# A graph layer on Trainium2: all chunks of the adjacency split in two parts, and the order of the engines' work changed

## What is computed

```python
h = jnp.maximum(_layernorm(x, axis=-1), 0.0)
A_fwd = [adj, adj, shifted]                      # shifted: identity rolled by one row
A_list = A_fwd + [transposed each] + [eye]       # 7 relations; shifted and eye are the same for all batches
HW  = einsum('bnf,rfo->rbno', h, W[:, :F]) + einsum('rd,rdo->ro', W_edges, W[:, F:])[:, None, None, :]
AHW = einsum('rbnm,rbmo->rbno', A, HW)
out = x + max(AHW over r) + b
```

## Time and profile before

| | us |
|---|---|
| median of 3 runs | 216.88 |
| lowest and highest | 216.61, 218.16 |
| profiled execution | 216.98 |
| its span (first to last instruction) | 215.3 |
| busy: TensorE, VectorE, ScalarE, GpSimd | 206.3, 177.0, 160.8, 95.9 |

### The profile page before, as it was taken

How to read it: one execution, slowest core, us unless ns; L and a number is a source line. 1 busy time by engine, 2 the same in 40 slices (tenths; PEclk the granted TensorE clock), 3 DMA queues, 4 the chain that set the end, 5 groups by cost and what they waited for, 6 DMA issues and landing times.

```text
span 215.3 us, 3420 instructions
## 1 busy us (share of the span) xinstructions
PE 206.3 (96%) x902; PEld 149.5 (69%) x902; DVE 177.0 (82%) x414; ACT 160.8 (75%) x431; POOL 95.9 (45%) x140
## 2 busy tenths in 40 slices
PE   7799779999999999999999999999999999999994
PEld 7456456777767777777767777776777777777772
DVE  3574997988889797988989798888979798888755
ACT  3779788697896969698796969689696969876220
POOL 3112946446172735527082644617273552718200
PEclk9999979999999999999999999999999999999998
DMA  5999995376693939678492938769393938610101
GB/s 175 313 345 370 376 362 199 108 292 245 202 336 93 380 79 313 215 253 283 156 355 69 374 127 295 241 198 335 86 384 89 342 130 253 234 53 0 50 0 49
DMA packets 31587, 47.14 MB, mean 219 GB/s; under 512 B 1632, under 2 KB 11088, under 8 KB 31568
## 3 DMA queue, kind: packets, MB, share of 16 engines
q1 hardware_dynamic: 31568, 46.92, 64.3%
HBM read 42.72 MB, written 4.19 MB: 218 GB/s over the span
## 4 chain that ended last, share of the span: by engine, by line
PE 84%; SPq 6%; DMA 5%; DVE 2%; issue 1%; ACT 1%; POOL 0%; DVEq 0%; ACTq 0%; POOLq 0%
PE bank_p L761 11%; PE bank_p L763 10%; PE bank_p L762 9%; PE bank_g L725 6%; PE bank_gT L704 6%; PE bank_g L730 5%; PE bank_g L729 5%; PE bank_g L736 5%; DMA adj_sb<-in_adj_dram 5%; PE bank_gT L716 5%; PE bank_gT L710 5%; PE bank_gT L709 4%; PE bank_p L751 3%; PE bank_p L679 3%; PE bank_p L671 3%; PE bank_g L762 2%
## 5 line engine op out<-in xcount | busy, mean ns | idle before, releaser
L321 POOL TENSOR_TENSOR a_lo<-adj_sb,a_hi 128x512 fp32r<-128x512 f32 x15 | 19.4, 1295 | 72.3 <-DVE h_lo L548 68.5
L579 DVE TENSOR_TENSOR best<-bank_p,best 128x512 f32<-128x512 f32 x48 | 33.2, 691 | 8.4 <-PE bank_p L763 7.3
L434 ACT ACTIVATE gT_hi<-bank_gT 128x512 fp32r<-128x512 f32 x16 | 9.6, 598 | 30.9 <-PE bank_gT L716 30.5
L576 DVE SCALAR_TENSOR_TENSOR best<-bank_p,c_col,best 128x512 f32<-128x512 f32 x32 | 24.0, 750 | 5.8 <-ACT best L453 5.1
L389 ACT ACTIVATE a_hi<-adj_sb 128x512 fp32r<-128x512 f32 x45 | 27.7, 620 | 1.3 <-DMA adj_sb<-in_adj_dram 1.3
L402 ACT ACTIVATE aT_hi<-adjT_sb 128x512 fp32r<-128x512 f32 x45 | 27.7, 620 | 0.0
L315 POOL TENSOR_TENSOR o_sb<-best,x_bias 128x512 f32<-128x512 f32 x15 | 20.0, 1332 | 15.8 <-DVE best L579 15.8
L418 ACT ACTIVATE h<-x_sb,shift,rstd 128x128 f32<-128x128 f32 x60 | 24.7, 497 | 1.4 <-DVE shift L528 1.4
L542 DVE TENSOR_TENSOR aT_lo<-adjT_sb,aT_hi 128x512 fp32r<-128x512 f32 x30 | 24.5, 854 | 0.0
L729 PE MATMUL bank_g<-aT_hi,h_hi 128*128 128x512 f32 x45 | 24.4, 541 | 0.0
L709 PE MATMUL bank_gT<-a_hi,h_hi 128*128 128x512 f32 x45 | 23.6, 525 | 0.0
(11 more groups left out here) (110 smaller groups left out, 501.8 us busy)
## 6 DMA issues: line engine op xcount, KB each, us to landing
adj_sb<-in_adj_dram SPq DMA_DIRECT2D x15, 1024.0 KB, 5.6
adjT_sb<-in_adjT_dram SPq DMA_DIRECT2D x15, 1024.0 KB, 5.6
xT_sb<-in_xT_dram SPq DMA_DIRECT2D x16, 256.0 KB, 5.9
x_sb<-in_x_dram SPq DMA_DIRECT2D x15, 256.0 KB, 6.1
out_dram<-o_sb SPq DMA_DIRECT2D x15, 256.0 KB, 5.9
adj_sb<-in_adj_dram SPq DMA_DIRECT2D x4, 256.0 KB, 3.4
adjT_sb<-in_adjT_dram SPq DMA_DIRECT2D x4, 256.0 KB, 4.8
w_sb<-in_W_dram SPq DMA_DIRECT2D x3, 128.0 KB, 4.5
```

Of the source, the lines that this page charges most:

```text
L579: op = nc.vector.tensor_tensor(best[q][:, :], product, best[q][:, :], ALU.max)
```

## The change

Chunk 0 is split as the others are: four chunks of a_hi, a_lo, aT_hi, aT_lo, h_hi and h_lo, and no float32 matmul from batch 1 on. VectorE makes two of the four low parts, GpSimd two. The copy into `summed` is gone for batches from 1 on; the same copy with its accumulator now writes a_hi. Then the order changes:
- TensorE does turn_sums behind aggregate, and the leading sums of the last batch's last product, in two halves, in begin_products.
- ScalarE makes sumsT behind g_hi. In batch 1 it does split_adj(2) behind the maximum's first term.
- VectorE does gT_lo and hT_lo ahead of a_lo(b+1). Batches 0 and 1 have an order of their own.
- GpSimd does part_sums(b+1) behind aT_lo(b+1), and finish(b-1) behind that.
- In batch 0 the layer norm goes in halves, the second half of x is loaded from ScalarE's queue, and the first aggregation comes ahead of the transposes.
- SP asks for adj and adjT of batch 2 before the second xT, and for x of batch 3 behind them.

```diff
-WHOLE = (0,)
-SPLIT = (1, 2, 3)
-NS = len(SPLIT)
-ND = NS - 1
+ND = 2
+NG = 2
+NS = ND + NG
-WARM_UP = 10
+WARM_UP = 9
...
             load_xT(0)
+            load_adj(2)
+            load_adjT(2)
             load_xT(1)
-            for b in range(B):
+            load_x(3)
+            for b in range(1, B):
+                if b + 1 < B:
+                    load_xT(b + 1)
                 if b + 3 < B:
                     load_x(b + 3)
                 if b + 2 < B:
                     load_adj(b + 2)
-                if b > 0:
-                    store(b - 1)
+                store(b - 1)
                 if b + 2 < B:
                     load_adjT(b + 2)
-                    load_xT(b + 2)
...
             split_adj_last(1)
             add_bias(0)
+            part_sums(1)
             split_adjT_last(1)
+            finish(0)
             add_bias(1)
             for b in range(1, B):
-                part_sums(b)
-                finish(b - 1)
+                if b >= 2:
+                    finish(b - 1)
                 if b + 1 < B:
...
                     split_adjT_last(b + 1)
+                    part_sums(b + 1)
...
+                if 2 <= b < B - 1:
+                    split_adj(b + 1)
                 split_gT(b)
                 split_hT(b)
-                copy_sumsT(b)
                 if b + 1 < B:
                     make_h(b + 1)
                 split_g(b)
+                copy_sumsT(b)
                 begin_best(b)
+                if b == 1:
+                    split_adj(b + 1)
...
             split_g_lo(0)
-            take_best(0, 1)
             split_h_lo(1)
             variance(2)
+            take_best(0, 1)
+            split_adj_lo(1)
             take_best(0, 2)
-            split_adj_lo(1)
+            scale_and_shift(2)
             for i in range(NH, NPROD):
                 take_best(0, i)
...
+            for c in range(C):
+                pe.wait_ge(ahi_ready, (b - 1) * NS + c + 1)
+                nc.tensor.matmul(bank_gT[:, 0:N], h_hi[q][:, c, :], a_hi[q][:, c, :], start=(c == 0), stop=False)
             pe.wait_ge(hlo_ready, b)
+            for c in range(C):
+                nc.tensor.matmul(bank_gT[:, 0:N], h_lo[q][:, c, :], a_hi[q][:, c, :], start=False, stop=False)
+            for c in range(C):
+                if c < ND:
+                    pe.wait_ge(alo_ready, (b - 1) * ND + c + 1)
                 else:
+                    pe.wait_ge(alo_last_ready, (b - 1) * NG + c - ND + 1)
+                last = nc.tensor.matmul(bank_gT[:, 0:N], h_hi[q][:, c, :], a_lo[q][:, c, :],
+                                        start=False, stop=(c == C - 1))
...
+                if b == B - 1:
+                    pe.wait_ge(best_begun, B)
+                    for nodes, to in zip(HALVES, last_banks):
+                        add_sums(NPROD - 1, to, nodes, start=True)
...
                 turn_h(b)
+                aggregate(b)
                 turn_sums(b)
-                aggregate(b)
```

More of the change, by code:

```diff
@@ L72, in gnn_kernel @@
         aT_lo = pair("aT_lo", [P, NS, N], F32R)
-        summed = pair("summed", [P, 2, C, N], mybir.dt.bfloat16)
+        summed = sb("summed", [P, 2, C, N], mybir.dt.bfloat16)
         hT_hi = sb("hT_hi", [P, N], F32R)
@@ L387, in split_adj @@
                     act.wait_ge(parts_lo, b - 1)
[L388 to L392, removed]
+                for c in range(C):
+                    last = nc.scalar.activation(a_hi[q][:, c, :], adj_sb[q][:, c, :], ACT.Copy,
                                                 accum_out=sums[q][:, 0, c:c + 1])
-                last.then_inc(sums_ready, 1)
+                    last.then_inc(ahi_ready, 1)
             def split_adjT(b):
@@ L400, in split_adjT @@
                     act.wait_ge(g_psum, b - 1)
[L401 to L405, removed]
+                for c in range(C):
+                    last = nc.scalar.activation(aT_hi[q][:, c, :], adjT_sb[q][:, c, :], ACT.Copy,
                                                 accum_out=sums[q][:, 1, c:c + 1])
-                last.then_inc(sums_ready, 1)
+                    last.then_inc(aThi_ready, 1)
             def make_h(b):
@@ L518, in variance, with first_variance, first_scale_and_shift @@
                 last.then_inc(aggr_done, 1)
+            def first_variance(i, stats_sem, aggr_sem):
+                dve.wait_ge(x0_in[i], 16)
+                for c in range(i * HALF, (i + 1) * HALF):
+                    last = nc.vector.bn_stats(stats[:, c, :], x_sb[0][:, c, :])
+                last.then_inc(stats_sem, 1)
+                dve.wait_ge(stats_sem, 1)
+                nc.vector.memset(wait_carrier[:, :], 0.0)
+                for c in range(i * HALF, (i + 1) * HALF):
+                    last = nc.vector.bn_aggr(mean_var[0][:, c, :], stats[:, c, :])
+                last.then_inc(aggr_sem, 1)
+            def first_scale_and_shift(i, std_sem, rstd_sem, shift_sem):
+                half = slice(i * HALF, (i + 1) * HALF)
+                dve.wait_ge(std_sem, 1)
+                nc.vector.reciprocal(rstd[:, half], std[:, half]).then_inc(rstd_sem, 1)
+                dve.wait_ge(rstd_sem, 1)
+                nc.vector.scalar_tensor_tensor(out=shift[:, half], in0=mean_var[0][:, half, 0], scalar=-1.0,
+                                               in1=rstd[:, half], op0=ALU.mult, op1=ALU.mult).then_inc(shift_sem, 1)
             def scale_and_shift(b):
                 dve.wait_ge(std_ready, b + 1)
-                if b >= 1:
-                    dve.wait_ge(h_ready, b)
+                dve.wait_ge(h_ready, b)
                 if b == 1:
@@ L787, in products_first @@
                 passes(4, bank_of[4][:, 0:N], start=True)
+                turn_sums(0)
                 product(0, 2)
```

188 lines of the change are left out of this document (101 added, 87 removed).

## The result

The changed kernel takes 219.38 us (median of 4 runs, 218.13 to 220.76) against 216.75 for the kernel before: ratio 1.0097, 95% interval 1.0052 to 1.0143. It is slower by 1%. The profiled execution took 219.48 us, with a span of 217.8. The changed kernel was not run again later; the kernel before was, beside the experiments, with medians of 217.43 (19 runs, for e1 to e4) and 216.99 (11 runs, for e5 to e8), and the ratios of the experiments are to those. One of the ten runs of e3 (220.46 us) was in a slower state and is left out of its ratio.

A forecast was written before the change was run, and what follows sets the result against it. It took TensorE, busy 96% of the span, as the bound. Start +2.3, steady batches +1.0 and end -0.5 make +2.8 on the profiled 216.98; with the median 0.1 lower, 219.7 us, range 213.5 to 224.

The forecast's parts named there:

- TensorE's own work: Both aggregations: float32r matmuls in place of the float32 chunk save 0.31 us a batch, TensorE alone at 11.98.
- Where o_sb lands: GpSimd, steady batches: o_sb is asked for 2.2 to 2.7 us behind aggregate_T's start, meeting VectorE's aT_lo pair.
- M + 10.2 - P: When o_sb is asked for, from aggregate_T's start: M is make_h's start, P the batch time; 2.2 to 2.7 us.
- What the meeting costs: VectorE, steady batches: o_sb holds up the second aT_lo; shift ends 2.67 us after the pair began, at 4.83.
- rival C: Steady batches: o_sb gets the port ahead of shift in each batch, pace 12.72, 223.9 us; chance 0.15.
- The new chain: ScalarE, steady batches: late shift puts sumsT at 8.21, product 2 waits 0.37 us; pace 12.35, taken as 12.37, +1.0.
- gT_lo and hT_lo ahead of a_lo: VectorE's new order, steady batches: both end before product 0 needs them, hidden with 0.35 us to spare.
- Start: First batches: TensorE's gain of about 1 us is lost on VectorE; aggregate_T(3) at 53.4, cost +2.3 us.
- The clock: Batch 1: granted clock falls again behind a wait of 2 to 3 us, hidden under the wait for aT_lo.
- End: Last batch: half products without leading sums and shorter aggregations give -0.5 us (0 to -0.9).
- A: Rival: TensorE stays the bound and o_sb misses the pair; 211.7 us, chance 0.15.
- B: Rival: the start is gained (-1.5 us), the steady part as forecast; 215.9 us, chance 0.17.

The follow-up runs named there:

- e1: The changed kernel with one more wait: GpSimd starts o_sb of the batch before only when shift of the next batch is done; 214.16 us, ratio 0.9848.
- e4: The changed kernel, VectorE in batch 0 doing the first maximum and a_lo of batch 1 ahead of the variance of batch 2; 216.71 us, ratio 0.9960.
- e5: The changed kernel with the edits of e1 and e4 together; 211.55 us, ratio 0.9726.
- e8: The kernel before with one wait added: in batches 3 to 13 GpSimd's o_sb starts only after the variance ahead of aT_lo; 223.95 us, ratio 1.0301.
- e3: The kernel before with only the sums moved: turn_sums behind aggregate, sumsT behind make_h and g_hi; 216.92 us, ratio 0.9986.
- e6: The changed kernel, from batch 3 on VectorE doing a_lo of the next batch ahead of gT_lo and hT_lo; 224.66 us, ratio 1.0345.
- e2: The changed kernel with shift made by four 128x1 operations reading one tensor each, in place of one reading two; 215.50 us, ratio 0.9915.
- e7: The changed kernel, from batch 3 on with turn_sums ahead of aggregate and sumsT ahead of make_h again; 221.71 us, ratio 1.0191.

## Why the prediction was right

The forecast was 219.7 us, slower by about 1.3%; measured 219.38. The mechanism is the forecast one: o_sb late, on the port that VectorE wants, shift late, then make_h and sumsT, and TensorE waits at product 2. Not all of it came as written, and two of the agreements below, the price of the meeting and the start, are in part luck.

- **TensorE's own work**: 0.31 a batch were forecast. The pace without waits is 11.93 (e1), so 0.36.
- **Where o_sb lands**: forecast M + 10.2 - P, 2.2 to 2.7. It starts at 118.43 - 114.91 = 3.5, since the small sums ahead of it wait 0.9 for the pair; without that wait it would be 2.6. The prediction said that no row shows whether the small sums queue too; they do.
- **What the meeting costs**: forecast is shift's end at 4.83, and it is 119.73 - 114.91 = 4.82. The size is right and its place is not. The step took the second aT_lo as the one that waits; that happens only in batch 4, and in batches 5 to 13 shift waits, for 1.1. A shift of over 1 us was the prediction's own sign of rival C, and it was seen; C's price was not (shift at 5.2, pace 12.72; the 5.2 has no working), since the pair is hardly delayed (1.30). That the forecast's price holds is luck, of a kind that the runs explain: o_sb follows the pair at once and lasts about as long in either place, so shift ends at 4.82 when it is hit itself and at 4.79 when the pair is (e6).
- **The new chain**: forecast pace 12.35, taken as 12.37 (the 12.55 among its ends has no working); measured 12.43. sumsT's end, forecast at 8.21, is at 123.06 - 114.91 = 8.15. From product 2 on it takes 4.23 (123.11 to 127.34), not the 4.14 that I took from before, where product 2 stood behind another product without a break. Over 12 batches +1.0 was forecast, +0.6 came, since batches 3 and 14 met no long hold-up (11.95 and 11.93).
- **gT_lo and hT_lo ahead of a_lo**: hidden, as forecast, and needed (e6).
- **Start**: forecast aggregate_T(2) at 38.7 and (3) at 53.4; measured 39.35 and 53.28. The variance of batch 4 was put at 42.0 and starts at 42.02. That they are so near is luck: it is a sum of terms with errors of both signs, a_lo's pair 2.5 as taken, aT_lo's 2.77 for 3.1, aggregate(1) at 27.8 for 28.6, and then waits of VectorE for ScalarE's g_hi (0.55) and first maximum (0.83), which I had not counted. In batch 2 the aT_lo pair meets GpSimd's own aT_lo, not o_sb, and takes 2.17. e4 shows what the order of batch 0 costs, together with the clock behind it; that a_lo between the maxima of batch 1 makes batch 2 long (13.93 against 12.27) is read from the timeline and was not tested.
- **The clock** fell again in batch 1, but was not hidden: the pair was ready at 30.45, and TensorE, at the lower level, reached aT_lo at 31.39. TensorE has no idle time from 27.82 to aggregate_T(2) at 39.35, so there it is the bound, and not VectorE's chain as forecast. The forecast had 10.1 from aggregate(1) to aggregate_T(2), and it took 11.53; since it had aggregate(1) 0.8 too late, only 0.65 is missing at aggregate_T(2). Against e4 and e5 the lower level costs about 1.4 in this stretch.
- **End**: forecast -0.5, measured -0.35.
- **Rivals**: A needs 11.93 in every batch, which e1 has and the changed kernel does not. B needs aggregate_T(3) near 49.5; even e5 has 50.04.

The Trainium skill, "SBUF — State Buffer", "SBUF: two separate sides", calls the shared port an exclusive lock that VectorE takes for two SBUF inputs against a GpSimd operation that reads SBUF. The runs agree: 1.24 for a 128x4 operation with two tensors, 0.58 for four with one tensor beside o_sb (e2), and GpSimd's small sums, which wait for the pair.

## What to carry to other kernels

Work added to an engine with idle time also moves everything behind it on that engine, and what moves may meet another engine's work: here two extra subtractions on GpSimd pushed an unrelated addition from 1.2 to 3.5 us behind the start of aggregate_T, onto VectorE's critical stretch. Look for short operations with a long duration in the timeline: such waiting counts as busy time. Here it was undone with one semaphore wait, which puts the addition where VectorE reads PSUM (e1). And a move made to shorten one chain (here sumsT's, to let make_h start sooner) should be checked against the latest time at which its new predecessor can end: it is free while shift is in time (e3), and passes the delay on to TensorE when shift is late. Putting it back does not help either, as long as the small sums are late too (e7).

## What was not expected of the hardware

What a meeting costs depends on which operation of GpSimd is queued when VectorE's first aT_lo ends. Batch 8, the pair and the two small sums one by one:

```profile
117.07 0.66 DVE L581 TENSOR_TENSOR aT_lo<-adjT_sb,aT_hi 128x512 fp32r<-128x512 f32 x1
117.14 0.69 POOL L308 TENSOR_TENSOR sum_parts<-sums,sum_parts 128x16 fp32r<-128x16 f32 x1
117.64 0.73 DVE L581 TENSOR_TENSOR aT_lo<-adjT_sb,aT_hi 128x512 fp32r<-128x512 f32 x1
117.79 0.69 POOL L308 TENSOR_TENSOR sum_parts<-sums,sum_parts 128x16 fp32r<-128x16 f32 x1
```

And the second aT_lo of batch 4, where o_sb (67.42 to 69.20) is queued in place of a small sum:

```profile
67.97 1.78 DVE L581 TENSOR_TENSOR aT_lo<-adjT_sb,aT_hi 128x512 fp32r<-128x512 f32 x1
```

In both the engines seem to take turns. Each small sum ends 0.1 behind the aT_lo that ran when it started (117.83 behind 117.73, 118.48 behind 118.37), and the second aT_lo is hardly longer for the small sum ahead of it (0.73, against 0.69 in e1). In batch 4, o_sb ends 1.15 behind the first aT_lo and the second aT_lo 0.55 behind o_sb. A small sum ahead of the second aT_lo thus costs 0.04, a 128x512 addition 1.1. That they take turns is read from these times, of which GpSimd's are rough, and was not tested by a run of its own.
